# Norms' scale and shift as two turned rows, attention values in five blocks a unit, deeper buffers and finer waits: a two-layer transformer and graph kernel

## The reference

```python
def _ada_ln(x, cond, W, b):
    ss = cond @ W + b
    scale, shift = jnp.split(ss[:, None, :], 2, axis=-1)
    return _ln(x) * (1.0 + scale) + shift

h = _ada_ln(x, cond, Wln1, bln1)
x = x + _attn(h, Wq, bq, Wk, bk, Wv, bv, Wo, bo)      # 16 heads of 32, 2048 keys
h = _ada_ln(x, cond, Wln2, bln2)
x = x + gelu(h @ W1 + b1) @ W2 + b2                   # 512 -> 2048 -> 512

self_feat = concat([x, q_exp], -1) @ W_self.T + b_self
for d in range(2):                                    # attention of each row to 20 nodes
    w = softmax(where(mask, qh @ kh / sqrt(dh), NEG) + label_bias)
    output = output + (w @ kv) @ Wout[d] + bout[d]
return x + relu(output)
```

## Time and profile before

| what | value |
|---|---|
| runs | 3121.56, 3128.03, 3131.30 us |
| profiled execution | 3132.72 us, span 3131.30 us |
| busy share of the span | PE 98%, PEld (weight loads) 68%, DVE 69%, POOL 49%, ACT 44% |
| costliest groups, busy us | DVE L397 1200.0; ACT L762 1031.0; POOL L861 995.9; PE L672 810.6; PE L384 803.5; PE L683 493.6 |
| HBM | 143.5 MB read, 75.5 MB written |

### The profile page before, as it was taken

How to read it: one execution, slowest core, us unless ns; L and a number is a source line. 1 busy time by engine, 2 the same in 40 slices (tenths; PEclk the granted TensorE clock), 3 DMA queues, 4 the chain that set the end, 5 groups by cost and what they waited for, 6 DMA issues and landing times.

```text
span 3131.3 us, 42990 instructions
## 1 busy us (share of the span) xinstructions
PE 3076.8 (98%) x16138; PEld 2144.6 (68%) x16138; DVE 2156.5 (69%) x3633; ACT 1388.4 (44%) x2703; POOL 1542.9 (49%) x655
## 2 busy tenths in 40 slices
PE   8999999999999999999999999899999999999999
PEld 7887655555555555555555546688888888778998
DVE  4457889998999999989999976443333333237776
ACT  2221466666666666666666672221111111013333
POOL 0000389889888898898898973200000000102222
PEclk9999999999999999999999999999999999899999
DMA  6674687879779788797887776520111110212221
GB/s 206 187 228 150 175 169 169 193 150 198 167 165 201 151 189 174 167 199 150 181 182 160 164 155 230 187 81 6 35 41 41 41 41 29 98 59 68 78 82 61
DMA packets 169366, 423.39 MB, mean 135 GB/s; under 512 B 18493, under 2 KB 60605, under 8 KB 141864
## 3 DMA queue, kind: packets, MB, share of 16 engines
q0 software_dynamic: 27744, 201.08, 31.7%
q1 hardware_dynamic: 139639, 214.07, 22.8%
q10 hardware_dynamic: 1776, 5.51, 0.7%
HBM read 143.51 MB, written 75.50 MB: 70 GB/s over the span
## 4 chain that ended last, share of the span: by engine, by line
PE 94%; DVE 2%; DMA 2%; issue 1%; POOL 1%; ACT 1%; SPq 0%; DVEq 0%; ACTq 0%; POOLq 0%
PE ps L384 16%; PE ps L672 15%; PE ps L683 15%; PE ps L1194 12%; PE ps L1181 11%; PE ps L460 5%; PE ps L1728 4%; PE ps L464 3%; PE ps L1745 3%; PE ps L689 2%; PE ps L1766 1%; PE ps L1045 1%; PE ps L1531 1%; PE ps L158 1%; PE ps L293 1%
## 5 line engine op out<-in xcount | busy, mean ns | idle before, releaser
L397 DVE TENSOR_REDUCE nmp<-ps 128x1 f32<-128x512 f32 x1966 | 1200.0, 681 | 108.2 <-PE ps L384 103.9
L762 ACT ACTIVATE pt<-ps 128x512 f32<-128x512 f32 x2048 | 1031.0, 625 | 458.7 <-PE ps L672 455.5
L861 POOL TENSOR_TENSOR pt<-pt 128x2048 f32<-128x2048 f32 x217 | 995.9, 4589 | 119.6 <-ACT pt L762 113.3
L672 PE MATMUL ps<-qs,ks 128*128 128x512 f32 x2048 | 810.6, 400 | 2.5 <-ACT pt L762 2.5
L384 PE MATMUL ps<-ks,qs 96*128 96x512 f32 x1966 | 803.5, 409 | 0.1
L384 PEld LDWEIGHTS ps<-ks,qs 96*128 96x128 f32 x1966 | 372.6, 190 | 265.3 <-DVE nmp L397 167.8
L683 PE MATMUL ps<-pt,vq 128*32 128x512 f32 x4096 | 493.6, 599 | 0.0
L672 PEld LDWEIGHTS ps<-qs,ks 128*128 128x128 f32 x2048 | 389.4, 191 | 96.2 <-ACT pt L762 19.5
L1181 PE MATMUL ps<-hpb,w 128*128 128x512 f32 x1536 | 382.6, 399 | 3.4 <-DMA x_d<-x 3.4
L1194 PE MATMUL ps<-w,gp 128*128 128x512 f32 x1536 | 380.5, 396 | 3.1 <-DVE gp L1305 3.1
L1303 DVE CAST gp<-g 128x512 fp32r<-128x512 f32 x128 | 61.7, 482 | 403.7 <-ACT g L1292 403.7
(11 more groups left out here) (169 smaller groups left out, 2874.9 us busy)
## 6 DMA issues: line engine op xcount, KB each, us to landing
pt<-pt POOLq DMA_DIRECT2D x189, 1024.0 KB, 8.7
qk_d<-st SPq DMA_DIRECT2D x128, 256.0 KB, 2.9
qs<-qk_d SPq DMA_DIRECT2D x87, 256.0 KB, 5.0
ks<-qk_d SPq DMA_DIRECT2D x42, 512.0 KB, 8.5
xina<-in_x SPq DMA_DIRECT2D x8, 1024.0 KB, 6.4
v_d<-vst SPq DMA_DIRECT2D x32, 256.0 KB, 3.1
vq<-v_d SPq DMA_DIRECT2D x32, 256.0 KB, 4.3
ao_d<-accs SPq DMA_DIRECT2D x32, 256.0 KB, 7.1
```

What stands on the lines that cost most here:

```text
L397: dve.tensor_reduce(nmp[:, n // 4, n % 4:n % 4 + 1], ps[:, ring.bank["max", u], :], AX.X, ALU.max, negate=True).then_inc(s_mr, 1)
L672: pe.matmul(ps[:, score_bank(n), :], ksb[w % 2][:, hh, 128 * kt:128 * kt + 128], qsb[:, v % 3, hh, :], start=True, stop=True).then_inc(s_s ...
L762: act.activation(pt[:, exp_slot(g), hh, :], ps[:, score_bank(n), :], ACT.Exp, scale=SCALE).then_inc(s_exp, 1)
L861: pool.tensor_tensor(accumulator(v, 0), accumulator(v, 0), pt[:, exp_slot(g), :, :], ALU.add).then_inc(s_add, 1)
```

## The change

It has five parts.

1. **Scale and shift.** `cond` is held in PE (two columns) and 512 columns of `Wln` move through it, so that scale is one row of 512 per batch and shift another (`pe_ss_row`). ACT and DVE copy the rows, PE turns them with eight small transposes (`pe_ss_turn`), DVE adds the biases in one instruction and 1.0 in another. The turned rows of chunk 0 use four banks.
2. **Attention.** In the first 31 units the values of two tiles after every eight steps become five blocks after steps 13, 26, 39, 52 and 64, of 2, 5, 3, 3 and 3 tiles (the first two are of the unit before). The sums stand after step 26, with all four reciprocals ahead of them on DVE, and the row of maxima is turned before step 50's maximum. The last unit keeps its blocks of two.
3. **Projection.** Eight buffers for the attention output and four for its halves; DVE splits tile t+3 before it waits for tile t's matmuls.
4. **Into feed-forward.** PE and ACT start the first block without waiting for the projection's last sums and stores; these are waited for one block later.
5. **Into the graph.** `pe_rows` comes ahead of `pe_vw`, and tile 0 is turned between the two `pe_vw`.

The core of the diff:

```diff
+BLOCKS = {13: (-2, -1), 26: (0, 1, 2, 3, 4), 39: (5, 6, 7), 52: (8, 9, 10), 64: (11, 12, 13)}
+SUMS_AT, ROW_AT = 26, 50
...
+        def pe_ss_row(i, half):
+            pe.wait_ge(s_sml[i], 32 - 16 * i)
+            for n in (2 * half, 2 * half + 1):
+                pe.wait_ge(s_wln[n], 16 * (i + 1))
+            for kk in range(NK):
+                m = pe.matmul(ps[0:B, 7 - half, :], condT[:, kk, :], wln[:, i, kk, D * half:D * half + D],
+                              start=(kk == 0), stop=(kk == NK - 1))
+            m.then_inc(s_ssp, 1)
...
+        def pe_ss_turn(i):
+            pe.wait_ge(s_sst, 2 * i + 2)
+            for n in range(2 * NK):
+                m = pe.transpose(ps[:, 7, 2 * n:2 * n + 2], ssT[:, n // NK, 128 * (n % NK):128 * (n % NK) + 128],
+                                 ident[0:B, 0:B])
+            m.then_inc(s_ssp, 1)
...
         def pe_qkv():
             step = 0
-            pe_scale_shift(0, 0, 7)
-            pe_scale_shift(0, 1, 6)
+            pe_ss_row(0, 0)
+            pe_ss_row(0, 1)
             pe.wait_ge(s_ident, 16)
             fa.pe_turn(0, 0, 0)
             fa.pe_turn(0, 1, 1)
-            pe_scale_shift(0, 2, 5)
-            pe_scale_shift(0, 3, 4)
-            fa.pe_turn(0, 2, 0)
-            fa.pe_turn(0, 3, 1)
+            pe_ss_turn(0)
+            fa.pe_turn(0, 2, 4)
+            fa.pe_turn(0, 3, 5)
             for ci in range(NC8):
                 hp = fa.hp[ci % 2]
                 if ci == 1:
-                    for k in range(NK):
-                        pe_scale_shift(1, k, 7 - k % 2)
+                    pe_ss_row(1, 0)
+                    pe_ss_row(1, 1)
                 for j in range(12):
+                    if (ci, j) == (1, 2):
+                        pe_ss_turn(1)
...
-            for p in range(NGRP // 2):
-                v, f = divmod(p, 8)
-                if f == 6 and v + 1 < NU:
-                    pe_row(v + 1)
+            for v in range(NU - 1):
+                for i in range(64):
+                    if i == ROW_AT:
+                        pe_row(v + 1)
+                    if EARLY - 2 + 64 * v + i < 64 * NU:
+                        pe_max(EARLY - 2 + 64 * v + i)
+                    pe_scores(16 * v + i // 4, i % 4)
+                    for kt in BLOCKS.get(i + 1, ()):
+                        if 16 * v + kt >= 0:
+                            pe_values(16 * v + kt)
+                    if i + 1 == SUMS_AT and v:
+                        pe_sums(v - 1)
+            for f in range(8):
+                g = 16 * (NU - 1) + 2 * f
                 for i in range(8):
-                    u = EARLY - 2 + 8 * p + i
-                    if u < 64 * NU:
-                        pe_max(u)
-                    pe_scores(2 * p + i // 4, i % 4)
-                if p:
-                    pe_values(2 * p - 2)
-                    pe_values(2 * p - 1)
-                if f == 2 and v:
-                    pe_sums(v - 1)
+                    pe_scores(g + i // 4, i % 4)
+                pe_values(g - 2)
+                pe_values(g - 1)
+                if f == 2:
+                    pe_sums(NU - 2)
...
+            for f in range(8):
...
+                if f == 1:
+                    dve_recip(v - 2)
...
         def sp_load_ao(t):
-            if t >= 3:
-                sp.wait_ge(s_ol, t - 2)
+            if t >= 8:
+                sp.wait_ge(s_ol, t - 7)
...
         def sp_out():
+            sp.wait_ge(s_sc, 64 * NU)
+            for t in range(3, 8):
+                sp_load_ao(t)
             for t in range(NT):
                 if t + 2 < NT:
                     sp_load_residual(t + 2)
-                if t + 3 < NT:
-                    sp_load_ao(t + 3)
+                if t and t + 7 < NT:
+                    sp_load_ao(t + 7)
...
         def pe_ff():
-            out_over(pe)
+            pe.wait_ge(s_accs, NU)
             pe_ff1(0)
             for q in range(NQ):
+                if q == 0:
+                    pe.wait_ge(s_oo, NT)
...
         def act_ff():
-            out_over(act)
-            act.wait_ge(s_bias, 96)
+            act.wait_ge(s_ol, NT)
+            act.wait_ge(s_bias, 80)
             for q in range(NQ + 1):
+                if q == 1:
+                    out_over(act)
+                    act.wait_ge(s_bias, 96)
...
-            for b in range(B):
-                pe_vw(b)
             for n in range(4):
                 pe_rows(n)
+            pe_vw(0)
+            pe_turn_x(0)
+            pe_turn_nz(0)
+            pe_vw(1)
```

More of the change, by code:

```diff
@@ L96, in __init__ @@
         self.uses = []
-        for p in range(NGRP // 2):
-            v, f = divmod(p, 8)
-            if f == 6 and v + 1 < NU:
[L100 to L103, removed]
-            if f == 2 and v:
-                self.use(("sums", v - 1))
+        for v in range(NU - 1):
+            for i in range(64):
+                if i == ROW_AT:
+                    self.use(("row", v + 1))
+                if EARLY - 2 + 64 * v + i < 64 * NU:
+                    self.use(("max", EARLY - 2 + 64 * v + i))
+                if i + 1 == SUMS_AT and v:
+                    self.use(("sums", v - 1))
+        self.use(("sums", NU - 2))
         self.use(("sums", NU - 1))
@@ L476, in act_qkv @@
         def act_qkv():
+            act_ss_row(0)
             for i in range(3):
                 for k in range(NK):
-                    if i == 0:
-                        fa.act_turn(0, k, k % 2)
+                    if i == 1 and k == 0:
+                        for n in range(NK):
+                            fa.act_turn(0, n, (0, 1, 4, 5)[n])
                     act_split(4 * i + k, wqkv[i][:, 0, k, :], wtmp[:, k, :], s_wt[k], 16 * (i + 1))
@@ L807, in dve_attention @@
         def dve_attention():
-            for p in range(NGRP // 2):
-                v, f = divmod(p, 8)
-                if f == 6 and v + 1 < NU:
-                    dve_row_split(v + 1, ring.bank["row", v + 1])
-                if v == NU - 1 and f in (0, 2):
-                    dve_split_wo(f)
-                    dve_split_wo(f + 1)
-                if f == 3 and v:
-                    dve_sums(v - 1)
-                for i in range(8):
-                    u = EARLY - 2 + 8 * p + i
+            for v in range(NU - 1):
+                for i in range(64):
+                    if i == ROW_AT:
+                        dve_row_split(v + 1, ring.bank["row", v + 1])
+                    u = EARLY - 2 + 64 * v + i
                     if u < 64 * NU:
@@ L1628, in dve_graph_shared @@
                                       gg[:, :, 0, kv_, c0:c0 + 160].bitcast(F32), ALU.subtract).then_inc(s_ggl, 1)
+            for n in range(4):
+                dve_rows(2 + n, n % 2, (5, 6, 3, 4)[n], D + 320 * (n // 2), 320)
+            weights_read(dve)
+            dve_zero(0)
+            dve_edges(0)
+            dve_turn_x(0)
             for b in range(B):
@@ L1770, in pe_graph @@
         def pe_graph():
-            for t in range(2):
-                pe_turn_x(t)
-                pe_turn_nz(t)
+            pe_turn_x(1)
+            pe_turn_nz(1)
             for t in range(-1, NT):
```

174 lines of the change are left out of this document (97 added, 77 removed).

## The result

The changed kernel takes 3156.49 us (median of four runs, 3155.54 to 3158.69) against 3127.06 us before (four runs, 3121.56 to 3131.30): ratio 1.0096, 95% interval 1.0079 to 1.0114. It is slower by 29 us. The profiled execution took 3155.9 us with a span of 3154.6, 23.3 longer than the span before.

What follows compares the result with a forecast made beforehand. PE, with 94% of the chain, was taken as the bound. Attention's +71.9 us and the other terms (-3, -3.8, -5.0, -14, -8.7, -8.5) gave +28.9: 3161.6 profiled, less 4.7, 3157 us median; range 3108 to 3186.

Steps and rivals of the forecast that it cites:

- The long runs: Attention: longer stretches of steps between blocks make PE wait for DVE's reductions, +2.37 us a unit, +71.9 us together.
- 0.45 a plain run: Attention: PE stops from the tenth step on, losing 0.13 us a step, 0.45 us by the thirteenth.
- 0.98 for the row: Attention, between steps 39 and 52: the row's maximum takes DVE 0.38 us and the turned row's bank 0.60.
- The 0.31 of a block: Attention: going into a block and out costs PE 0.31 us; three blocks fewer save 0.93 us a unit.
- Its other use, 9.6 us more for the row's turning: Attention: by the tiling rule the row's turning adds 31 x 0.31 = 9.6 us, kernel 3167 us.
- the first: Rival, attention: four banks do not bind, only switches count; each unit gains 0.93 us, kernel 3056 us; chance 0.10.
- The second, a row that hides: Rival, attention: the row costs no more than plain steps, sums nothing; 29 us less than forecast, 3128 us; chance 0.14.
- The third: Rival, attention: the exponentials' sum comes late, PE waits 0.60 us a unit, 18 in all, 3175 us; chance 0.08.
- The fourth: Rival, projection: paced by transfers, not buffers, so the 14 us do not come, 3171 us; chance 0.08.
- Second norm, start, graph: Three terms outside attention: second norm -5.0 us, start -3.8, the way into the graph -8.5.
- The last unit: Attention's end: reciprocals stand together, PE's 2.04 us wait for an exponential and slower matmuls go, -3 us.
- Into feed-forward: From projection to feed-forward's second product: first block starts at once, second gelu waits for its bias; -8.7 us, between -10 and -5.

Runs made afterwards that it cites:

- the second experiment: The changed kernel with the row of maxima turned before step 52's maximum, behind the block, instead of before step 50's: 3147.63 us, ratio 1.0069.

## Why the prediction was right

3157 was forecast and 3156.5 measured, but half a microsecond is luck. On the profiled executions the sum was +28.9 and +23.3 was measured, 3161.6 against 3155.9: terms up to 4.2 us too high, less others up to 2.9 too low. What made up for the rest is the step to the median. The forecast took off 4.7, because the profiled execution before lay that much above its median; the changed kernel's lay 0.6 below.

- **The long runs.** Right in mechanism and nearly in size. 0.45 a plain run was 0.44 (6.73 us for 13 steps and 0.12 on leaving the block, less 6.10 and the 0.31); 0.2 behind the sums was 0.20 (6.93 against 6.73); 0.98 for the row was 0.98 (7.71 against 6.73). Maxima begin to stand further apart behind the tenth with four banks, behind the fifth with three, and nowhere in a plain run with reductions of half the columns. The sum of 2.37 a unit came out at 2.19, since the pieces were a hundredth or two smaller each, and the longer blocks (2.71 for three tiles, 6.15 for five and the sums) 0.12 together under what 1.74 for two gives; and 71.9 came out at 67.7.
- **What the row pays.** The total was right, its division only partly: the second experiment shows that 0.66 of the 0.98 stays when the row moves behind the block, the maximum's 0.38 and about 0.29 of a bank's turn. The 0.38 itself is right (in that experiment 0.98 lies between two maxima where 0.60 is usual), but the prediction's working for it, 0.69 and five times 0.60, gives the end of a reduction and so only 0.28; six starts at 0.60 give 0.37.
- **The 0.31 of a block.** Right: undisturbed units with halved reductions are 0.9 us shorter than with eight blocks. The Trainium skill, "TensorEngine Tiling (Array Packing)", Key Properties, speaks of a drain when the tiling mode changes; 0.18 on going in (6.28 - 13 x 0.469) and 0.12 on leaving (1.86 a block, less 1.74) agree with it. Its other use, 9.6 us more for the row's turning, did not come: the row's 0.98 is what its maximum and its bank were to cost without it, and with halved reductions, where no bank holds PE up in a plain run, the run with the row is 0.11 longer than others (6.39 against 6.28) and not 0.31.
- **The rivals.** Four banks do bind, so the first fell. The second, a row that hides, fell with 7.71; its 29 us left the 0.2 behind the sums in, although it says that the sums cost nothing, and with that it would be 35. The third is real, but behind the stop. The fourth fell: the projection gained 15.4.
- **Second norm, start, graph.** Within 0.7. The granted clock is full with 512 columns in place of two, as forecast. The 0.44 for such an instruction is what the earlier trace rows gives (3.53 for eight), and the second norm's sixteen took 7.03 for 7.06; its eight turnings took 0.65 where 1.2 was taken. The start's sixteen took 9.39: the first five distances are 0.81 to 0.86 us, those from 15.56 on 0.43. The granted clock on record is 1.00 there throughout, so no row says what held the first ones up.
- **The last unit.** The step that failed: "I take -3 us". The wait of the earlier trace rows went, and 2.01 us appeared at 1936.89, where DVE's additions stand ahead of the first split, with a slow first tile (4.57) behind it. In the version with the weights split earlier it is gone.
- **Into feed-forward.** 7.4 for 8.7, within its bounds. The second gelu waits for the bias, as forecast, but until 11.6 us behind the projection's end instead of 10.5 (ACT in time):

```profile
2049.52 0.69 ACT L1349 ACTIVATE g<-ps,b1c 128x512 f32<-128x512 f32 x1 [2.07 <-DMA b2B<-in_b]
```

The last addition of the projection waits for its residual, and with it the stores, which the bias' load stands behind on SP.
- **Not forecast:** 3.0 us in feed-forward's body. They lie near its end, in a stretch that begins with 32 matmuls of two moving columns (L1225, now L1277) and in which the clock falls in both kernels. PE in time, before:

```profile
2683.95 4.81 PE L1225 MATMUL ps<-condT,wcT 128*128 128x2 f32 x32
...
2727.05 4.59 PE L1181 MATMUL ps<-hpb,w 128*128 128x512 f32 x12
```

and after:

```profile
2718.68 3.63 PE L1277 MATMUL ps<-condT,wcT 128*128 128x2 f32 x32
...
2760.18 3.01 PE L1233 MATMUL ps<-hpb,w 128*128 128x512 f32 x12
```

The granted clock beside the 32 is 0.74 before and 1.00 after, beside the twelve 0.62 and 1.00. By their starts these two places differ by 1.2 and 1.6 us, and twelve matmuls soon behind the 32 by 0.4. The change does not touch them, and the 32 take 3.6 us in the version with eight blocks and 4.5 in the one with the row behind the block. Why the clock falls earlier in one execution than in another was not tried.

Of the versions that reduce whole banks, those of the changed kernel with seven or eight blocks beat both kernels: eight blocks with all other parts take 3088 us, and with the weights split early some 3084 to 3085.

## What to carry to other kernels

A block that interrupts a stream of matmuls can be the pause in which the engine behind it catches up. Before blocks are merged, work out from the two rates and the number of buffers at which step the stream would stop; here that was the tenth, and each thing that held DVE early in a run moved it forward. And a consumer that takes its next input ahead of finishing the last output needs buffers to match: the same order was free with eight buffers and cost 95 us with three.

## What the runs showed of the hardware that was not expected

In the last unit DVE's casts and subtractions within SBUF took seven to thirteen times their usual time while POOL was adding. DVE and POOL in time, changed kernel:

```profile
1890.35 5.63 DVE L495 TENSOR_TENSOR wo<-wtmpo,wo 128x512 fp32r<-128x512 f32 x1
...
1916.17 0.69 DVE L495 TENSOR_TENSOR wo<-wtmpo,wo 128x512 fp32r<-128x512 f32 x1
```

```profile
1890.13 5.29 POOL L900 TENSOR_TENSOR pt<-pt 128x2048 f32<-128x2048 f32 x1
```

The same instruction takes 5.63 us beside POOL's addition and 0.69 without it, and it ends at 1895.98, just behind that addition (1895.42). Casts of the same size took 4.16 and 5.27 us instead of 0.41. The reductions of banks, which read PSUM, did not slow down: seven from 1880.67 on, beside another addition of POOL, took 4.28 us, 0.60 apart as usual. The Trainium skill, "Trainium Architecture — The Big Picture", What this means for kernel authors, says that DVE and GpSimd (POOL here) contend for a shared pair of ports, by a lock; these rows agree.
